# Loading x in two parts, transposing by quarters and alternating PSUM pairs in a one-layer attention and ternary feed-forward kernel

## The reference

```python
x: (4, 4096, 1024); w_lin: (16 * 31, 1024); weight: (1024, 1024)
a = layernorm(x)
w = softmax(einsum('btc,fc->btf', a, w_lin) as (b, t, 16 heads, 31 taps))
x = x + (for each head h of 64 columns: out[t] = sum over k of w[t, h, k] * a[t + k - 30])
b = layernorm(x)
d = 0.7 * mean(abs(weight)); q = +1 where weight > d, -1 where weight < -d, else 0
x = x + einsum('bsd,od->bso', b, q * alpha) + bias
```

## Time and profile before

| | us |
|---|---|
| median of 2 runs | 542.44 (540.86 to 544.02) |
| the profiled execution | 538.86 |
| its span on the slowest core | 537.1 (cores: 518.6 to 537.1) |
| TensorE busy | 170.9 |
| VectorE busy | 131.8 |
| ScalarE busy | 70.5 |

### The profile page before, as it was taken

The page is one execution under the profiler, slowest core; times in us unless marked ns, Lnnn a source line. Parts: engine busy times, 40 slices in busy tenths (PEclk is TensorE's granted clock), DMA queues, the critical chain, the costliest instruction groups (busy, mean ns, idle before and its releaser), DMA issues.

```text
span 537.1 us, 2881 instructions; the slowest of 8 cores (518.6 to 537.1 us)
## 1 busy us (share of the span) xinstructions
PE 170.9 (32%) x934; PEld 94.8 (18%) x940; DVE 131.8 (25%) x250; ACT 70.5 (13%) x78; POOL 5.8 (1%) x8
## 2 busy tenths in 40 slices
PE   0002000000000533444754362640000476767670
PEld 0000000000000211111454362640000132323220
DVE  0007227910000222222263280750000021111110
ACT  0000571044600100000000000006330000000000
POOL 4000000000000000000000000000000000000000
PEclk9999999999999877666755555555555699999897
DMA  8997000026589377333389989802449403030303
GB/s 216 268 278 261 0 1 0 0 84 204 187 153 172 78 157 157 80 78 78 78 147 195 208 141 173 158 0 78 156 117 179 95 1 156 0 156 1 157 0 157
DMA packets 83878, 64.50 MB, mean 120 GB/s; under 512 B 67344, under 2 KB 68368, under 8 KB 83864
## 3 DMA queue, kind: packets, MB, share of 16 engines
q1 hardware_dynamic: 72904, 38.08, 30.9%
q10 hardware_dynamic: 9856, 25.24, 17.9%
q0 software_dynamic: 1104, 1.02, 1.5%
HBM read 23.14 MB, written 25.40 MB: 90 GB/s over the span
## 4 chain that ended last, share of the span: by engine, by line
DMA 40%; PE 17%; DVE 13%; ACT 10%; SPq 7%; issue 5%; DVEq 3%; ACTq 3%; POOLq 0%
DMA stage<-wpad 11%; DMA wet<-stage 10%; DMA wlTb<-wlT 8%; PE ps_ff L565 5%; PE ps_ff L563 5%; PE ps_at L550 5%; SPq L177 4%; DMA out<-outst 4%; SPq L208 3%; DMA xn2d<-xn2r 3%; ACT xn L456 3%; DMA xn1d<-xn 3%; ACT xn2r L504 2%; DVE outst L371 2%; DVE statsw L135 2%
## 5 line engine op out<-in xcount | busy, mean ns | idle before, releaser
L531 PE MATMUL ps_wp<-wlTb,xn1T 128*128 128x496 bf16 x128 | 42.7, 510 | 162.0 <-DMA xn1T<-xn1d 114.2
L565 PE MATMUL ps_ff<-wtern,xn2T 128*128 128x512 bf16 x128 | 53.1, 415 | 68.9 <-DMA xn2T<-xn2d 67.1
L550 PE MATMUL ps_at<-wins,wet 128*64 128x64 bf16 x512 | 50.8, 305 | 41.1 <-DMA wet<-stage 27.8
L563 PE MATMUL ps_ff<-wtern,xn2T 128*128 128x512 bf16 x122 | 50.7, 416 | 26.8 <-DVE outst L371 26.8
L550 PEld LDWEIGHTS ps_at<-wins,wet 128*64 128x64 bf16 x512 | 50.2, 216 | 42.0 <-issue 42.0
L371 DVE TENSOR_TENSOR outst<-ps_ff,xs 128x512 f32<-128x512 f32 x32 | 20.6, 686 | 128.6 <-PE ps_ff L567 108.4
L531 PEld LDWEIGHTS ps_wp<-wlTb,xn1T 128*128 128x128 bf16 x128 | 15.6, 125 | 188.7 <-issue 184.1
L331 DVE TENSOR_REDUCE sumc<-wpad 128x16 f32<-128x496 bf16 x16 | 10.7, 667 | 114.4 <-ACT wpad L427 114.4
L563 PEld LDWEIGHTS ps_ff<-wtern,xn2T 128*128 128x128 bf16 x128 | 13.5, 105 | 118.2 <-issue 107.2
L342 DVE TENSOR_TENSOR xs<-ps_at,xs 128x1024 f32<-128x1024 f32 x16 | 19.6, 1222 | 39.4 <-PE ps_at L550 39.1
L427 ACT ACTIVATE wpad<-ps_wp,cstb 128x496 bf16<-128x496 f32 x16 | 10.0, 672 | 119.2 <-DMA stage<-wpad 84.2
(11 more groups left out here) (73 smaller groups left out, 63.4 us busy)
## 6 DMA issues: line engine op xcount, KB each, us to landing
stage<-wpad ACTq DMA_DIRECT2D x16, 512.2 KB, 7.3
xs<-x SPq DMA_DIRECT2D x1, 8192.0 KB, 51.3
wins<-xn1d ACTq DMA_DIRECT2D x16, 512.0 KB, 8.1
out<-outst SPq DMA_DIRECT2D x4, 2048.0 KB, 6.6
wTf<-wT ACTq DMA_DIRECT2D x1, 4096.0 KB, 40.7
xn1d<-xn ACTq DMA_DIRECT2D x4, 1024.0 KB, 4.6
xn2d<-xn2r SPq DMA_DIRECT2D x4, 1024.0 KB, 4.5
wlTb<-wlT POOLq DMA_DIRECT2D x1, 992.0 KB, 41.5
```

The source lines that it names most:

```text
L531: mm = tensor.matmul(pw[:, 0:F], xn1T[:, cc * T + i * 128:cc * T + (i + 1) * 128], wlTb[:, cc * F:(cc + 1) * F], start=(cc == 0), stop=(cc ...
L550: mm = tensor.matmul(pa[64 * jj:64 * jj + 64, h * R:(h + 1) * R], lhsT, rhs, start=True, stop=True)
L563: tensor.matmul(ps_ff[0][:], lhs, wtern[:, cc * C:cc * C + 512], start=(cc == 0), stop=False)
L565: tensor.matmul(ps_ff[1][:], lhs, wtern[:, cc * C + 512:cc * C + 1024], start=(cc == 0), stop=False)
```

## The change

Four edits. The load of x is split into two DMAs of eight tiles each, `ldx` and `ldx2`, both ahead of the halo. VectorE takes the statistics of halo and tiles 0 to 7 before the weight work, behind waits for `ldx` and for the halo (`ldh`). Both sets of 8 transposes of 2048 rows become 4 times 8 of 512 rows, each four-tile quarter behind the wait for its own write and with a semaphore of its own (`x1ts`, `xnts`), for which TensorE waits at every fourth tile. The FFN alternates between `ps_ff` and `ps_wp`, so TensorE waits for the eviction of the tile before the last. Besides, the second `wet` transpose names the wait for `tern` again, which the first has met.

```diff
@@ sync
+        sync.dma_start(
+            bass.AP(xs, 8 * C, [[NT * C, 128], [C, 8], [1, C]]),
+            bass.AP(x_d, 8 * 128 * C, [[C, 128], [128 * C, 8], [1, C]]),
+        ).then_inc(sems["ldx2"], 16)
         sync.dma_start(halox[:], halo_d[:]).then_inc(sems["ldh"], 16)
 
         if level >= 2:
-            for w_ in range(1, 5):
-                sync.wait_ge(x1ds[w_], 16)
-            for cc in range(8):
-                src_ = bass.AP(xn1_d, 32 * C + 128 * cc, [[C, T], [1, 128]])
-                sync.dma_start(xn1T[:, cc * T:(cc + 1) * T], src_, transpose=True).then_inc(x1t, 16)
+            for q_ in range(4):
+                sync.wait_ge(x1ds[1 + q_], 16)
+                for cc in range(8):
+                    src_ = bass.AP(xn1_d, (32 + 512 * q_) * C + 128 * cc, [[C, 512], [1, 128]])
+                    sync.dma_start(xn1T[:, cc * T + 512 * q_: cc * T + 512 * (q_ + 1)],
+                                   src_, transpose=True).then_inc(x1ts[q_], 16)
...
-            for cc in range(8):
-                if cc == 0:
-                    for w in range(4):
-                        sync.wait_ge(x2ws[w], 16)
-                src = bass.AP(xn2_d, 128 * cc, [[C, T], [1, 128]])
-                sync.dma_start(xn2T[:, cc * T:(cc + 1) * T], src, transpose=True).then_inc(sems["xnt"], 16)
+            for q_ in range(4):
+                sync.wait_ge(x2ws[q_], 16)
+                for cc in range(8):
+                    src = bass.AP(xn2_d, 512 * q_ * C + 128 * cc, [[C, 512], [1, 128]])
+                    sync.dma_start(xn2T[:, cc * T + 512 * q_: cc * T + 512 * (q_ + 1)],
+                                   src, transpose=True).then_inc(xnts[q_], 16)
@@ vector
         vector.drain().then_inc(sems["vprep"], 1)
+        vector.wait_ge(sems["ldx"], 16)
+        vector.wait_ge(sems["ldh"], 16)
...
+        stats_tile(vector, halox[:, 0:512], halox[:, 512:C], 0, 32)
+        for i in range(8):
+            stats_tile(vector, xs[:, i * C:i * C + 512], xs[:, i * C + 512:(i + 1) * C], 1 + i, 128)
+        stats_batch(vector, 0, 9, scm1[:, 0:9], scv1[:, 0:9], scq1[:, 0:9], scn1[:, 0:9])
+        vector.drain().then_inc(sems["ln1s"], 1)
         vector.wait_ge(sems["ldwl"], 16)
...
+                fb = [ps_ff[0], ps_ff[1]] if i % 2 == 0 else [ps_wp[0], ps_wp[1]]
...
-                        ps_ff[hf][:], xs[:, i * C + hf * 512:i * C + hf * 512 + 512],
+                        fb[hf][:], xs[:, i * C + hf * 512: i * C + hf * 512 + 512],
@@ tensor
-            tensor.wait_ge(x1t, 128)
-            for i in range(NT):
+            for i in range(NT):
+                if i % 4 == 0:
+                    tensor.wait_ge(x1ts[i // 4], 128)
...
-            tensor.wait_ge(sems["xnt"], 128)
...
-                if i >= 1:
-                    tensor.wait_ge(sems["outs"], 2 * (i - 1) + 2)
+                if i % 4 == 0:
+                    tensor.wait_ge(xnts[i // 4], 128)
+                if i >= 2:
+                    tensor.wait_ge(sems["outs"], 2 * (i - 2) + 2)
+                fb = [ps_ff[0], ps_ff[1]] if i % 2 == 0 else [ps_wp[0], ps_wp[1]]
```

More of the change, by code:

```diff
@@ L113, in build_nc @@
     sems = {}
-    for s in ["lds", "ldx", "ldh", "ldw", "ldxt", "ldwl", "ldba", "x1d", "vprep", "gz", "vsq", "vabs", "mrt", "mrv", "mrf", "vcell",
+    for s in ["lds", "ldx", "ldx2", "ldh", "ldw", "ldxt", "ldwl", "ldba", "x1d", "vprep", "gz", "vsq", "vabs", "mrt", "mrv", "mrf", "vcell",
               "scell", "bcv", "tch", "tern", "ln1s", "rinv1", "cols1", "xn1a", "wp",
@@ L119, in build_nc @@
     winbs = [stack.enter_context(nc.semaphore(f"winb{i}")) for i in range(16)]
-    x1t = stack.enter_context(nc.semaphore("x1t"))
+    x1ts = [stack.enter_context(nc.semaphore(f"x1t{i}")) for i in range(4)]
     xnts = [stack.enter_context(nc.semaphore(f"xnt{i}")) for i in range(4)]
@@ L185, in _ @@
                            wpad[0:8, 0:1536]).then_inc(sems["stl"], 16)
-            for b in range(N_WB if level >= 4 else 2):
+            for b in range(N_WB if level >= 4 else 1):
                 sync.wait_ge(stgs[b], 32)
-                if b == 0:
+                if b <= 1:
                     sync.wait_ge(sems["tern"], 8)
@@ L227, in _ @@
         gpsimd.drain().then_inc(sems["gz"], 1)
-        finals = [("ldx", 16), ("ldh", 16), ("ldw", 16), ("ldwl", 16), ("ldba", 32)]
+        finals = [("ldx", 16), ("ldx2", 16), ("ldh", 16), ("ldw", 16), ("ldwl", 16), ("ldba", 32)]
         fin = {1: (sems["xn1a"], 17), 2: (sems["wnorm"], 16), 3: (wetbs[1], 16),
-               4: (sems["x1"], 16), 5: (sems["xnt"], 128), 6: (sems["od"], 64)}[level]
+               4: (sems["x1"], 16), 5: (xnts[3], 128), 6: (sems["od"], 64)}[level]
         gpsimd.wait_ge(fin[0], fin[1])
@@ L235, in _ @@
         if level >= 2:
-            gpsimd.wait_ge(x1t, 128)
+            for s_ in x1ts:
+                gpsimd.wait_ge(s_, 128)
             for s_ in x1ds[1:]:
@@ L251, in _ @@
                 gpsimd.wait_ge(s_, 16)
-            gpsimd.wait_ge(sems["xnt"], 128)
+            for s_ in xnts:
+                gpsimd.wait_ge(s_, 128)
         if level >= 6:
@@ L279, in _ @@
         vector.drain().then_inc(sems["vprep"], 1)
+        vector.wait_ge(sems["ldx"], 16)
+        vector.wait_ge(sems["ldh"], 16)
+        vector.memset(statsw[:, 0:12], 0.0)
+        vector.drain()
+        stats_tile(vector, halox[:, 0:512], halox[:, 512:C], 0, 32)
[3 more added lines that the diff above has]
+        vector.drain().then_inc(sems["ln1s"], 1)
         vector.wait_ge(sems["ldwl"], 16)
@@ L303, in _ @@
                                  wet[:, WET_ROWS_PAD:WET_ROWS_PAD + C], ALU.add).then_inc(sems["tern"], 1)
-        vector.wait_ge(sems["ldx"], 16)
-        vector.wait_ge(sems["ldh"], 16)
-        vector.memset(statsw[:, 0:12], 0.0)
-        vector.drain()
-        stats_tile(vector, halox[:, 0:512], halox[:, 512:C], 0, 32)
-        for i in range(8):
-            stats_tile(vector, xs[:, i * C:i * C + 512], xs[:, i * C + 512:(i + 1) * C], 1 + i, 128)
-        stats_batch(vector, 0, 9, scm1[:, 0:9], scv1[:, 0:9], scq1[:, 0:9], scn1[:, 0:9])
-        vector.drain().then_inc(sems["ln1s"], 1)
+        vector.wait_ge(sems["ldx2"], 16)
         for i in range(8, NT):
@@ L558, in _ @@
             for i in range(NT):
-                if i >= 1:
-                    tensor.wait_ge(sems["outs"], 2 * (i - 1) + 2)
+                if i % 4 == 0:
[3 more added lines that the diff above has]
+                fb = [ps_ff[0], ps_ff[1]] if i % 2 == 0 else [ps_wp[0], ps_wp[1]]
                 for cc in range(8):
                     lhs = xn2T[:, cc * T + i * 128:cc * T + (i + 1) * 128]
-                    tensor.matmul(ps_ff[0][:], lhs, wtern[:, cc * C:cc * C + 512],
+                    tensor.matmul(fb[0][:], lhs, wtern[:, cc * C:cc * C + 512],
                                   start=(cc == 0), stop=False)
-                    tensor.matmul(ps_ff[1][:], lhs, wtern[:, cc * C + 512:cc * C + 1024],
+                    tensor.matmul(fb[1][:], lhs, wtern[:, cc * C + 512:cc * C + 1024],
                                   start=(cc == 0), stop=False)
-                tensor.matmul(ps_ff[0][:], onesbr[0:1, :], biasb[0:1, 0:512],
+                tensor.matmul(fb[0][:], onesbr[0:1, :], biasb[0:1, 0:512],
                               start=False, stop=True).then_inc(sems["ffn"], 1)
-                tensor.matmul(ps_ff[1][:], onesbr[0:1, :], biasb[0:1, 512:1024],
+                tensor.matmul(fb[1][:], onesbr[0:1, :], biasb[0:1, 512:1024],
                               start=False, stop=True).then_inc(sems["ffn"], 1)
```

4 lines of the change are left out of this document (2 added, 2 removed).

## The result

The changed kernel takes 515.81 us (median of 11 runs, 502.41 to 529.54), the kernel before 538.91 (10 runs, 534.14 to 549.61). The ratio is 0.9368, 95% interval 0.9288 to 0.9448: 5.5 to 7.1% faster. The forecast was 485 with a range of 475 to 500, a gain of 57.9 us; the medians differ by 23 us. The ratio compares only undisturbed executions, of which the changed kernel had two (502.41 and 505.04 us), and stands for 34 us. The direction was right, and between four and six tenths of the gain came. The profiled execution took 509.96 us.

The account below looks back on a forecast made before the run. No engine was taken as the bound: stages follow one another, and at every seam one thing ends last. +9.6 - 17.7 - 18.2 - 31.6 = -57.9 us gave 481.0 against the profiled run, 485 against the median; range 475 to 500.

Parts of the forecast that it names:

- Part 1: Start: statistics of the first half ahead of the weights make VectorE wait for the halo; +9.6 us, bounds +8.6 to +10.6.
- The rival with the halo early: Start: halo and first half of x land by about 29, so statistics gain 13.2 us; 462 us, chance 0.05.
- Part 2: First transposes by quarters: only the last quarter stays before the first exp; -17.7 us, bounds -21.6 to -10.8.
- I take a quarter, 0.73 us: Price of a 512-row transpose, scaled by rows from 2048 rows at 2.94 us; bounds 0.5 and 1.03.
- about every 11 us at first: First seam: spacing of the normalised quarters' writes, under which the first three quarters of transposes were to hide.
- The write that it named as a sign of being wrong: First seam: xn1d writes that took 4.6 us landing after 8 would show the forecast wrong.
- Part 3: Second transposes by quarters, before the FFN: first FFN matmul at 404.7, not 422.91; -18.2 us, bounds -21.8 to -13.
- Part 4: FFN with two pairs of banks: first matmul to last output 71.6 us, not 103.2; -31.6 us, bounds -33 to -25.
- The milder form of the slower one: Both sets of transposes: each 512-row transpose costs 1.5 us; 503 us in all, chance 0.08.
- the slower one: Both sets of transposes: each costs by the instruction, still 2.94 us; 567 us in all, chance 0.05.
- The clock rival: FFN: denser matmuls on all cores hold TensorE's clock below full; 494 us at 0.81, chance 0.10.
- TensorE's gap: FFN sign: one TensorE gap of about 1.5 us in four tiles, while VectorE waits for the output DMA.

Follow-up runs that it names:

- e5_halo_first: The changed kernel with the halo's load issued first on SyncE's queue, ahead of both loads of x: 490.59 us, ratio 0.9078.
- e2_first_quarters: The kernel before with only the first set of transposes cut into quarters (32 of 512 rows): 542.34 us, ratio 1.0103.
- e4_banks: The kernel before with only the two pairs of banks in the FFN: 516.02 us, ratio 0.9442.
- e7_out_on_act: The changed kernel with the four output DMAs issued by ScalarE instead of SyncE: 503.76 us against 538.66 for the kernel before.
- e9_best: The changed kernel with halo first, fills before transposes, ScalarE issuing output tile by tile, second transposes between the xn2d writes: 438.43 us, ratio 0.8244.
- e10_weights_first: e9_best with VectorE taking the weights first and the loads of x issued only after both weight loads landed: 431.15 us, ratio 0.8025.

## Why the prediction was too far out

**Part 1, +9.6 us: right in its mechanism, a little high.** +8.1 in the changed kernel, +7.7 alone, just under its lower bound of 8.6. The halo did hold VectorE (51.98). The rival with the halo early, 462, did not come, and e5_halo_first shows that even then x would have held it at 38 to 45.

**Part 2, -17.7 us: this step failed; it gave -3.1.** The step was "I take a quarter, 0.73 us", with 1.03 as its upper end. It drew a line through transposes of 4112 and 2048 rows down to 512, and took "no fixed part shows" for "there is none". Up to 1024 rows there is a floor of 1.23 us (1.24 for 256 rows, 1.32 for 1024). With 1.27 us from one to the next, 32 of them need some 40 us of SyncE, not 23. The third quarter no longer hid either: the last two writes are issued 5.2 us apart (151.08, 156.25) and 8 transposes take 10 us, so 16 stood in line. This spacing was in the trace of the kernel before, where the write ahead of the one at 143.66 is 5.1 us earlier (core 0):

```profile
138.53 0.39 ACTq L461 DMA_DIRECT2D xn1d<-xn  x1
```

The forecast went by "about every 11 us at first" and let only one quarter stand in line.

The floor is not all of it. On the means over the cores, had the write of quarter 2 landed 32.7 us after the first normalise as before, the first exp would have come 20.3 us (16 transposes) and 3.1 us (from there to the first exp) after it, at 56.2. That is an estimate from these rows, and 9.9 less than the 66.1 of the kernel before. The floor thus took about 10 of the 19.7 us that the forecast had before contention. The second term that was too small is contention, the early transposes beside the writes, which e2_first_quarters shows against the kernel before: in the changed kernel the write of quarter 2 lands 5.7 us later (38.5), and the 16 transposes take 1.1 longer. That is 6.8 us, where the forecast had 2 and at most 4.5. The write that it named as a sign of being wrong, 4.6 before, took 8.23.

**Part 3, -18.2 us: right in kind, off in size.** -14.1. The forecast had 5.3 us for eight transposes; at 1.27 each they take 10.2, 4.9 more, which is all of the difference of 4.1.

**Part 4, -31.6 us: right alone, and halved in company; this step left something out.** e4_banks gives -29.6. In the changed kernel it is -16.3, since the output is issued from the queue that holds 32 transposes. The forecast called the later quarters hidden, and looked only at who waits for the transposes, not at what is queued behind them. At 0.73 us each they would have been out by 418 and the output would not have noticed; on core 3 of the changed kernel they were out at 439.95. The same wrong price was thus paid three times: about 10 us in part 2, 4 in part 3 and 10.3 in part 4, the last by e7_out_on_act.

**The rivals.** The milder form of the slower one, 1.5 us a transpose and 503, was the nearest in mechanism and in time, and had 0.08. It, too, left out the output behind the transposes. The rule of the Trainium skill that small transfers should be coalesced ("DMA: Bandwidth & Descriptors") pointed the right way: the trace now agrees that at 256 and 512 rows a transpose is mostly overhead, since 1024 rows cost hardly more. The fixed cost of 2.0 us, which the same page of the Trainium skill ("Anatomy of one DMA") gives for DMAs issued by GpSimd, is not what was paid. SyncE paid 1.23 for issuing one, and the landing lay beside it (2.9 us in the median). The clock rival fell: 1.00 on all eight cores of e9_best with TensorE busy all the time. The 13/16 level that "TensorE: Matmul & The Clock Gate" of the Trainium skill states for dense matmuls on several cores of a die does not show in that stretch, nor in the changed kernel's from 452 to 466, at 1.00; the granted clock of every core in all thirteen traces is either 0.50 or 1.00. What the clock did lose it lost behind TensorE's waits (0.50).

**The signs.** Named in advance and seen: VectorE's start (51.98), the weights' square (65.6 on core 3), and VectorE waiting for the output. Named and missed: the price of a transpose (1.23, not 0.5 to 1), the first exp (181.89, not 169), the first FFN matmul (411.2 on core 3, 11.7 us earlier and not 26) and TensorE's gap (11.24, not 1.5).

**The range.** It was made from bounds that all took the same scaling for granted. Put 1.27 us into the forecast's own working and change nothing else. The write of quarter 2 has landed at 138.5 + 9.6 + 4.6 = 152.7, and the first exp comes at 152.7 + 20.3 + 3.5 + 2 = 178.5, so part 2 is -8.3. Part 3 is -13.3. The output goes out at 394.8 + 40.6 = 435.4 and not when tile 3 is evicted, at 428.7, so part 4 is -24.9. With +9.6 the sum is -36.9 and the time 505.5, outside the range of 475 to 500. One term, priced at its floor, moves the forecast 20 us, and contention as measured would move it another 5, to 510. The good end of part 2 was also set too near: it keeps 2.0 us for the landing of the fills, which the text lets be about nothing.

## What to carry to other kernels

- Cutting a DMA into pieces multiplies what its issuing costs, and the cost of a piece can have a floor that the long ones don't show. Where the trace has no short one, the upper bound for a piece is the whole, not the share.
- Work that is moved beside other transfers slows them: here that cost 6.8 us, more than three times the forecast, and it adds up over every transfer in the chain.
- Ask of each queue what stands behind the instructions that a change multiplies. Here it was three small fills and the output, neither of them mentioned in the change. On the mean of the cores, moving the fills alone brought the end 16.6 us forward and moving the output alone 10.1, where the whole change brought 31.2.
- Work that is moved earlier takes on the waits of its inputs. The statistics moved in front of the weights waited for the last load in the queue. Letting the weights' loads go first (e10_weights_first) brought the first normalise 15.5 us forward, though only 7.3 us of it reached the time.
